# Attention with routed experts on one Trainium2 core: logits by quarters, choice of experts spread out, two row buffers, normalisation on VectorE, maxima split before their transposition

## The reference

```python
x = x + xattn(layernorm(x), ctx, ctx)                  # phase_project, with q, k, v of the next layer
y = layernorm(x)
q, k, v = (y @ qw + qb), (y @ kw + kb), (y @ vw + vb)  # 16 heads of 32, 4 groups of k and v
attn = softmax(q k^T / sqrt(32))                       # all 2048 keys
src = y + (attn v) @ ow + ob                           # phase_attend
src = norm1_w * src * rsqrt(mean(src * src) + 1e-6)
probs = sigmoid(src @ gate_w)                          # 8 experts
sel = top_k(probs, 2)                                  # rank of a row within its expert, capacity 1280
xe[slot of (row, expert)] = src                        # each row is sent to its 2 places
ye = gelu(xe @ w1) @ w2                                # phase_experts
out = x + norm2_w * rmsnorm(src + sum_k w_k ye[slot])  # phase_combine
```

## Time and profile before

| what | us |
|---|---|
| median of 3 executions | 3563.71 (3556.47 to 3568.64) |
| the profiled execution | 3558.09 |
| its span in the trace | 3556.2 |
| phase_attend in it | about 430 to 2440 |
| six middle chunks of phase_attend | 1474.09, so 245.7 a chunk |

### The profile page before, as it was taken

The page is one execution under the profiler, slowest core; times in us unless marked ns, Lnnn a source line. Parts: engine busy times, 40 slices in busy tenths (PEclk is TensorE's granted clock), DMA queues, the critical chain, the costliest instruction groups (busy, mean ns, idle before and its releaser), DMA issues. The chain is left out here.

```text
span 3556.2 us, 47058 instructions
## 1 busy us (share of the span) xinstructions
PE 3164.5 (89%) x16936; PEld 2047.9 (58%) x16936; DVE 2184.4 (61%) x3738; ACT 1615.2 (45%) x3252; POOL 2012.8 (57%) x912
## 2 busy tenths in 40 slices
...
GB/s 103 154 161 138 167 103 135 59 42 52 49 44 51 49 34 78 22 60 51 31 60 41 54 43 34 13 27 141 72 72 90 78 87 71 94 88 72 27 242 212
DMA packets 199217, 284.62 MB, mean 80 GB/s; under 512 B 86295, under 2 KB 91415, under 8 KB 196485
## 3 DMA queue, kind: packets, MB, share of 16 engines
...
...
## 5 line engine op out<-in xcount | busy, mean ns | idle before, releaser
L1132 DVE TENSOR_REDUCE p_mxp<-p_ps_a 128x1 f32<-128x512 f32 x2048 | 1282.0, 681 | 251.7 <-PE p_ps_a L1308 238.5
L1052 ACT ACTIVATE p_PR<-p_ps_b 128x512 f32<-128x512 f32 x2048 | 1065.5, 603 | 787.0 <-PE p_ps_b L1322 773.4
L924 POOL TENSOR_TENSOR p_PP<-p_PP,p_PR 128x2048 f32<-128x2048 f32 x224 | 1026.7, 4583 | 37.8 <-ACT p_PR L1052 14.8
L1308 PE MATMUL p_ps_a<-p_KS,p_QS 96*128 96x512 f32 x2048 | 837.7, 441 | 33.9 <-DMA p_KS<-kh_d 17.0
L1322 PE MATMUL p_ps_b<-p_QS,p_KS 98*128 98x512 f32 x2048 | 761.7, 419 | 6.8 <-ACT p_PR L1052 5.9
L920 POOL TENSOR_TENSOR p_PP<-p_PR 128x2048 f32<-128x2048 f32 x128 | 586.8, 4584 | 214.6 <-ACT p_PR L1052 190.2
L1308 PEld LDWEIGHTS p_ps_a<-p_KS,p_QS 96*128 96x128 f32 x2048 | 391.0, 195 | 476.8 <-DVE p_mxp L1132 311.5
...
L1328 PE MATMUL p_ps_pv<-p_PR,p_VS 128*32 128x512 f32 x4096 | 525.3, 614 | 0.0
L1322 PEld LDWEIGHTS p_ps_b<-p_QS,p_KS 98*128 98x128 f32 x2048 | 391.8, 192 | 204.6 <-ACT p_PR L1052 119.2
L1606 ACT ACTIVATE p_hf<-p_ps_h 128x384 f32<-128x384 f32 (+1 forms) x256 | 112.0, 438 | 558.6 <-PE p_ps_h L83 553.1
L81 PE MATMUL p_ps_h<-p_xTh,p_w1h 128*128 128x256 f32 (+1 forms) x1024 | 322.2, 315 | 1.2 <-DVE p_xTl L1651 1.2
...
## 6 DMA issues: line engine op xcount, KB each, us to landing
...
```

What stands on the lines that cost most here:

```text
L924: nc.gpsimd.tensor_tensor(PP[:, buf, :, :], PP[:, buf, :, :], PR[:, tile_at(u, tile), :, :], ALU.add).then_inc(add_made, 1)
L1052: nc.scalar.activation(PR[:, tile_at(u, kt), j, :], ps_b[:, n % BK, :], ACT.Exp, scale=SCALE).then_inc(ex_made, 1)
L1132: nc.vector.reduce_max(mxp[:, a // (S // CH), a % (S // CH):a % (S // CH) + 1], ps_a[:, bank, :], AXX).then_inc(a_read, 1)
L1308: nc.tensor.matmul(ps_a[:, bank, :], QS[0:96, g, j, t * P:(t + 1) * P], KS[0:96, g, kb * CH:(kb + 1) * CH], start=True, stop=True).then_in ...
```

## The change

Five edits, all in phase_attend:

1. **Logits by quarters.** L becomes four matmuls, one for each quarter of D: the stationary operand is `gw`, widened to 32 columns of which 8 hold weights, the moving operand is `srT` (128x512), and each quarter lands in its own 32 partitions of one bank. DVE copies the bank to `lgq`; a new letter N, in group 2, key tile 1, sums the quarters by four matmuls of 8 columns against `fold`, which POOL builds once at the start.
2. **The choice of experts spread out.** The copy of the logits stands at N, the maxima in key tile 1, their indices in 2, the one-hot tiles in 3, their sum `sel` in 4. `topf` and both one-hot tiles are now in SBUF.
3. **Two row buffers.** `SR` is doubled, by the chunk's parity. Four sends stand in group 3, behind adds 1, 3, 5 and 7; the other four in group 0 of the chunk after, behind the same adds.
4. **The norm on VectorE.** POOL's L937 and ACT's L1075 go; DVE multiplies by root and weights in one instruction for each row tile, in group 1, key tiles 6 to 9.
5. **Maxima split early.** DVE makes high and low part straight behind `mxv`, in SBUF (`mhl`), a tensor_scalar and a scalar_tensor_tensor; M transposes both together (8 columns in place of 4), and DVE copies the bank once to `mrow`.

```diff
-    EXTRA = {0: {11: "O", 13: "O", 15: "O"}, 1: {1: "O", 10: "R", 11: "R", 12: "R", 13: "R"}, 2: {0: "L", 8: "K"}, 3: {}}
+    EXTRA = {0: {11: "O", 13: "O", 15: "O"}, 1: {1: "O", 10: "R", 11: "R", 12: "R", 13: "R"}, 2: {0: "L", 1: "N", 8: "K"}, 3: {}}
...
-    POWER_AT, NORM_AT, SCALE_AT = (1, 2), {(1, 1): (0, 1), (1, 3): (2, 3)}, {(1, 8): (0, 1), (1, 9): (2, 3)}
+    POWER_AT, SCALE_AT = (1, 2), {(1, 6): 0, (1, 7): 1, (1, 8): 2, (1, 9): 3}
...
-    EXP_AT, INVERT_1_AT, INVERT_2_AT, SUM_AT = 1, 3, 7, 12
-    SENDS = {(3, 0): (0,), (3, 1): (1,), (3, 2): (2,), (3, 4): (3,), (3, 5): (4,), (3, 6): (5,), (3, 7): (6,), (3, 9): (7,)}
+    TOP_AT, INDEX_AT, EXP_AT, HOT_AT, INVERT_1_AT, SELECT_AT, INVERT_2_AT, SUM_AT = 1, 2, 2, 3, 4, 4, 7, 12
+    SENDS = {(3, 1): 0, (3, 3): 1, (3, 5): 2, (3, 7): 3}
+    LATE_SENDS = {(0, 1): 4, (0, 3): 5, (0, 5): 6, (0, 7): 7}
...
-                nc.gpsimd.tensor_tensor(SR[:, t, :], SR[:, t, :], norm_row[:], ALU.mult).then_inc(normed, 1)
...
-                nc.scalar.activation(SR[:, t, :], SR[:, t, :], ACT.Copy, scale=sr_rstd[:, t:t + 1]).then_inc(sr_made, 1)
...
                     nc.vector.reduce_max(mxv[:].rearrange("p t j -> p (t j)"), mxp[:], AXX).then_inc(mxv_made, 1)
+                    dve.wait_ge(mxv_made, u + 1)
+                    nc.vector.tensor_scalar(mhl[:, :, 0, :], mxv[:], -1.0, None, ALU.mult).then_inc(mh_made, 1)
+                    dve.wait_ge(mh_made, u + 1)
+                    nc.vector.scalar_tensor_tensor(mhl[:, :, 1, :], mxv[:], -1.0, f32(mhl[:, :, 0, :]), ALU.mult, ALU.subtract).then_inc(ml_made, 1)
...
-                nc.vector.tensor_scalar(mh[:], ps_a[0:G, bank, :], -1.0, None, ALU.mult).then_inc(mh_made, 1)
-                dve.wait_ge(mh_made, u + 1)
-                nc.vector.scalar_tensor_tensor(ml[:], ps_a[0:G, bank, :], -1.0, f32(mh[:]), ALU.mult, ALU.subtract).then_inc(ml_made, 1)
-                dve.wait_ge(ml_made, u + 1)
-                dve.sem_inc(a_read, 1)
+                nc.vector.tensor_copy(mrow[:], ps_a[0:2 * G, bank, :]).then_inc(a_read, 1)
...
+            def scale(c, t):
+                dve.wait_ge(rstd_made, c + 1)
+                nc.vector.scalar_tensor_tensor(SR[:, c % 2, t, :], SR[:, c % 2, t, :], sr_rstd[:, t:t + 1], norm_row[:],
+                                               ALU.mult, ALU.mult).then_inc(sr_made, 1)
...
+                nc.vector.tensor_copy(topf[:], topi[:, :, 0:2]).then_inc(route, 1)
                 dve.wait_ge(route, ROUTES * c + 2 * TT + 1)
...
+                for k in range(2):
+                    nc.vector.tensor_tensor(oh[:, k, :, :], topf[:, :, k:k + 1].broadcast_to((P, TT, E)), per_expert(iota_e[:]), ALU.is_equal).then_inc(route, 1)
+
+            def select(c):
+                dve.wait_ge(route, ROUTES * (c + 1))
+                nc.vector.tensor_tensor(sel[:], oh[:, 0, :, :], oh[:, 1, :, :], ALU.add).then_inc(sel_made, 1)
```

More of the change, by code:

```diff
@@ L724, in slot_of, with m_slot @@
         return count, count % AK
+    def m_slot(c, g):
+        return next(slot_of(c, g, kt, pos)[0] for kt in range(KT) for pos, x in enumerate(ORDER[g][kt]) if x == "M")
     def last_slot(c, what):
@@ L1013, in body @@
                             finish(c - 1)
-                        for t in NORM_AT.get((g, n), ()):
-                            norm(c - 1, t)
                         if (g, n) in SENDS:
-                            send(c - 1, SENDS[g, n])
+                            send(c - 1, (SENDS[g, n],))
+                        if (g, n) in LATE_SENDS and c > 1:
+                            send(c - 2, (LATE_SENDS[g, n],))
             body(0, first=True)
@@ L1022, in _ @@
             body(NC - 1)
-            for t in range(TT):
-                norm(NC - 1, t)
+            send(NC - 2, sorted(LATE_SENDS.values()))
             norm_power(NC - 1)
             weigh(NC - 1)
-            rank(NC - 1, TAIL + 2 * TT + 2)
+            rank(NC - 1, TAIL + 2 * TT + 3)
             finish(NC - 1)
@@ L1103, in body @@
                             squares(c - 1, SQUARES_AT[g, kt], projected[SQUARES_AT[g, kt]])
-                        if (g, kt) in SCALE_AT and not first:
-                            for t in SCALE_AT[g, kt]:
-                                scale(c - 1, t)
                         if g == 2 and not first and kt == EXP_AT:
@@ L1117, in _ @@
                 squares(NC - 1, t, TAIL + t + 1)
-            for t in range(TT):
-                scale(NC - 1, t)
             sigmoid_exp(NC - 1)
@@ L1257, in body @@
                                 low(u - 1, (g - 1) % KV)
+                        if (g, kt) in SCALE_AT and not first:
+                            scale(c - 1, SCALE_AT[g, kt])
                         if g == 2 and not first:
+                            if kt == TOP_AT:
+                                top_two(c - 1, last_slot(c, "N"))
+                            if kt == INDEX_AT:
+                                top_indices(c - 1)
+                            if kt == HOT_AT:
+                                one_hot(c - 1)
+                            if kt == SELECT_AT:
+                                select(c - 1)
                             if kt == INVERT_1_AT:
```

143 lines of the change are left out of this document (81 added, 62 removed).

## The result

The changed kernel takes 3699.58 us in the median of four executions (3694.91 to 3700.84), the kernel before 3560.09 (3555.07 to 3568.64) in four taken with it. The ratio is 1.0387, 95% interval 1.0362 to 1.0411: slower by 139.5 us. The prediction said slower, 3817, with 3610 to 3900 as its range.

The account below looks back on a forecast made before the run. The prediction took PE, a queue in fixed order, as the bound. A middle chunk's terms summed to 30.4, six to 182; with 37, 31, 5 and -2 that is +253, giving 3817 us, range 3610 to 3900.

Parts of the forecast that it names:

- The prediction's own sign of being wrong: Profile after: if L1136 has a mean under 0.5 us, units stay near 55 and only L1174 is left.
- both long: Profile after: L1134 and L1136 with means of 3 to 5 us; the first case, 3817, chance 0.62.
- only L1136: Profile after: of L1134 and L1136 only L1136 is long; the second case, 3671, chance 0.22.
- split: At mxv: instructions wait for POOL's adds; 0.3, 7.2, 7.2, 2.5 by group, 17.2 us a chunk.
- norm: Group 1, key tiles 6 to 9: price 2.98 less 1.27 idle plus 4.85 of waits, 6.6 us a chunk.
- choice: Group 2: cast waits half an add (2.3), first one-hot a whole one (4.6); +6.9 us a chunk.
- logits: L and N: 1.7 less work and 1.7 less clock loss; -3.4 us a chunk.
- sends: At the D of group 3: moving half the sends removes POOL's lateness and its clock loss; -4.9 us a chunk.
- new half-clock stretches: Behind four new stops a chunk (groups 1 and 2 at mxv, scale, choice): 2.0 each, +8 us.
- The row that decides: DVE beside POOL: each waits for whole instructions of the other, read from L527, L472 and L1824.
- The rival at 3671: At split and choice: only two-input instructions wait, tensor_scalar and cast run at once; +107, 3671, chance 0.22.
- The rival on the other side: At mxv: nothing waits, each split costs 0.5 us of idle DVE; -60, 3504, chance 0.12.

Follow-up runs that it names:

- edit 1 alone: Against the kernel before: logits by quarters, choice in one piece at N in PSUM, sends at old places, norm and split as before; 3534.97 us, ratio 0.9923.
- edits 1 and 3: Against the kernel before: logits by quarters, two row buffers with spread sends, choice in one piece at N in PSUM; 3496.42 us, again 3494.92.
- the split from PSUM: Edits 1 and 3 with the maxima split early, mxv in the PSUM bank in place of SBUF; 3491.38 us, again 3484.02, ratio 0.9788 against the kernel before.

## Why the prediction came out as it did

Direction and range were right, and so was the kind of mechanism; the time was 117 us too high, and the forecast loss of 253 came out as 139.5. The prediction's own sign of being wrong came in: L1136 has a mean of 0.31 us, under the 0.5 that it named. What it said would then follow did not (units near 55 and only L1174 left), since L1134 waited. The case "both long" did not happen, nor did the rival's "only L1136"; the kernel did a third thing. In us per middle chunk, measured as the difference over the six-chunk window between the kernels with and without an edit (1589.9 for the changed kernel; 1508.7, 1559.0 and 1543.2 with split, norm and choice undone; 1475.4 before, 1454.1 with edit 1 alone, 1423.8 with edits 1 and 3):

| term | forecast | measured, clock included |
|---|---|---|
| split | 17.2 | 13.5 |
| norm | 6.6 | 5.2 |
| choice | 6.9 | 7.8 |
| logits | -3.4 | -3.5 |
| sends | -4.9 | -5.1 |
| new half-clock stretches | 8.0 | in the rows above |
| sum | 30.4 | 17.9; the whole change 19.1 |

- **The row that decides.** Right. The wait for whole instructions of POOL, read off from L527, L472 and L1824, holds for tensors of 128x16, and for a tensor_scalar and a cast with one input in SBUF. The rivals in which small instructions or one-input instructions run free are refuted by L1134 and L1208. The Trainium skill (SBUF — State Buffer, Who interferes with whom) says that whoever issues first holds the pair of SBUF ports that the two engines share for the whole instruction. The trace agrees, now also at 128x16 (3.07 us median in place of 0.17).
- **Maxima split early: the step that failed.** "The scalar_tensor_tensor, which waits for it on a semaphore, finds the second add begun": it doesn't, it starts 34 ns behind the first one's end, and the add 0.12. In the plain unit that is one wait (3.4) in place of two (8.2). The split's term was 152 us with chunks 0, 1 and 7, before its share of the clock; undoing it gives 102 with the clock. Where the wait is shorter than I had it, in groups 1 and 2 (3.1 and 5.0 by the units of chunk 2 in place of 7.2), the error is this step. In group 3 I was too low: 2.5 forecast, 4.5 to 6.2 measured. There L1134 meets an add from its start (1187.19 beside 1187.15) and waits it out, 4.51. The extra 5 us for group 0 of chunk 1 did not come: L1134 waits 0.64 there. The gain at M, 0.95, is what key tile 15 shows (5.12 to 4.16).
- **The norm.** 6.6 a chunk without the clock; 5.2 measured in the window, 43 us in all by undoing it. The waits, 2.05, 1.2, 1.6 and 0 forecast, were 2.1, 1.0, 1.3 and 0 (2.88, 1.78, 2.03 and 0.74 us long in chunk 2).
- **The choice.** 6.9 a chunk, 48; 53 measured. A cast of 2.1 and one-hot of 4.5, but it was the second one-hot that waited and not the first. That the sum is close is luck in this part.
- **Logits.** -3.4 a chunk and 2 at the end, -26; -25 measured.
- **Sends.** -4.9 a chunk, -29 in six; -30 measured in the same six, and 3 more in chunk 7, which the forecast left out. POOL was not late in group 0. A send's price was added wrongly (0.99 and 0.17 are 1.16, not 1.13); nothing hangs on it.
- **Stops and clock.** Against edits 1 and 3 alone, which run the same 7706 matmuls in the six chunks, the changed kernel has 97.0 us more of PE's idle time and 69.1 more of its busy time, at a clock of 0.94 in place of 1.00: 16.2 and 11.5 a chunk. The forecast had 30.7 for the stops (split, norm and choice) and 8 for the clock. So it priced the stops at nearly twice what PE idled, and the clock too low, as far as the longer busy time is the clock.
- **The ends.** Chunk 0 lost 18 us where 37 was forecast, the split's error four times over. Chunk 7 lost 10 where 31 was forecast; there the last split costs nothing, since no score maxima follow it.

The parts as measured by undoing them sum to 102 + 43 + 53 - 25 - 39 = +134, against 139.5, so little is left between them.

The rival at 3671 ended closer, 29 us off where the forecast was 117 off, with a wrong cause (the tensor_scalar runs free, the second instruction waits once). It gives nearly the right length for a pair, one wait, by the wrong instruction. That two causes give nearly one price is why L1134 and L1136 had to be looked at apart. The rival on the other side, 3504 with nothing waiting, is near what edits 1 and 3 give alone (3496). With the split from PSUM beside them it is 3484.
